# One constant row written on chip instead of sent, and the mask transfers moved behind a weight load, in a one-core attention and feed-forward block

## The chip, the cores and the metric

One core of a Trainium2 chip runs the whole block in one launch. The metric is the device time of that core in microseconds; lower is better. The median of three runs before the change is 766.67 us (765.58 to 767.1).

## The reference

The input x is 1024 tokens of 512 features, in float32. The block is two residual steps, each modulated by vectors from a conditioning row c:

```
mod = silu(c) @ wmod, cut into sa, ca, ga, sb, cb, gb
h = layernorm(x) * (1 + ca) + sa
x = x + ga * attention(h)
h = layernorm(x) * (1 + cb) + sb
x = x + gb * ffn(h)
```

`attention` has 32 heads. Queries come from a latent of 128 numbers per token (RMS-normalised), keys and values from a latent of 32, and a rotary part of 64 numbers is shared by all heads on the key side. The scores are causally masked, go through a softmax, and the values are summed and projected back to 512. `ffn` is a gated feed-forward net with integer weights and 1376 hidden features.

## The kernel before

The program for each engine is written out by hand, with semaphores between the engines. SyncE (SP) issues every transfer, in the order in which the function `sp_program` names them; a wait in it holds everything behind it.

The work has these stages. In the input stage (about 12 to 54 us) the eight tiles of 128 tokens are normalised, turned and projected, which makes the latents and the keys. Then the 32 heads are taken as eight groups of four. For the first group a stage of its own (about 60 to 88 us) finds the row maxima of the scores: TensorE (PE) multiplies queries by keys piece by piece (`maxima_part`, L736), and VectorE reduces each piece. The list `FIRST_MAXIMA` gives the order. Before its first piece PE runs eight matmuls whose result nobody uses (`keep_busy`, L780). After that eight windows of about 57 us follow, one per group (from 90 to about 550 us): each computes the scores of its group, takes exponentials and sums values, and beside this finds the maxima of the next group and makes the queries of the group after that. Last come the output projection and the feed-forward net.

Queries are made four heads at a time on all partitions (tile `TQ`) and are then moved by transfers, one per head and per half of the tokens, into `Q`, where the contraction rows 0 to 95 lie on partitions 0 to 95 (`send_queries`, L531). `maxima_part` waits for each head's transfer (`S_.q`). PE takes its work strictly in order.

The causal mask within a diagonal tile is done by the matmul itself: the contraction is made longer by 32 rows, on partitions 96 to 127. Those rows of `KL`, `KH` and of the two parts of `Q` (high and low, `hl` 0 and 1) hold the constants that `mask_rows` makes. Row 96 (`KR`) of `KH` is all ones, and row 96 of the low part of `Q` takes the negated row maxima of the group, one value per query (`send_maxima`, L540, from `NM`), so that the same matmul subtracts them.

The constants come in one small load to `mask_raw`, GpSimd (POOL) casts them to `mask_made` (L1656), and four transfers spread them along the rows: one each for `KL` and `KH` (8 copies of 128 columns per row) and one for each part of `Q` (32 copies) (`send_mask_rows`, L546). `Q` has two slots, for even and odd groups. The odd slot is filled in the first window by two transfers from the even slot (`copy_mask_rows`, L550). `load_weights(1)` (L521 to L523) fetches the weights of group 1 after POOL has finished with those of group 0 (`S_.wl`, L1669). POOL's first instructions are memsets: `ident`, `ones`, two of `eps`, then `oner` (L1643), `twice` (L1645) and further constants.

Of the kernel before, what the change touches and what calls it, by code (L numbers as in the profile page):

```python
# [7 lines left out]
F32 = mybir.dt.float32  # L8
# [6 lines left out]
P = 128  # L15
# [5 lines left out]
KR = 2 * HALF + L  # L21
# [50 lines left out]
def mask_levels():  # L72

    sizes = [2] * (MASK_ROWS * 2 - 3) + [3] * 3
    starts = [sum(sizes[:n]) for n in range(len(sizes))]
    assert sum(sizes) == P - 1
    return list(zip(starts, sizes))


def mask_rows():  # L80

    k = np.zeros((2, L, P), np.float32)
    q = np.zeros((2, L, P), np.float32)
    for n, (start, size) in enumerate(mask_levels()):
        hide, keep = (30, 45) if size == 2 else (20, 32)
        row = (n // MASK_ROWS, 1 + n % MASK_ROWS)  # L90
        for i in range(size):
            q[row + (start + i,)] = -2.0 ** (hide - i * (hide + keep))
            k[row + (start + 1 + i,)] = 2.0 ** (i * (hide + keep))
        k[row + (slice(start + size + 1, P),)] = 2.0 ** ((size - 1) * (hide + keep))
    k[1, 0] = 1.0
    return np.concatenate([k, q]).transpose(1, 0, 2)


# [406 lines left out]
def sp_program(nc, t, out, M, S_):  # L505
    sp = nc.sync

    def wait_free(engine, key):
        engine.wait_ge(S_.free[TURN[key] % 3], freed(key))

    def load_columns(n):
        sp.dma_start(M.mod_c[n], t["wmod_c"][n]).then_inc(S_.wm[n], 16)

    def load_rows(n):
        sp.wait_ge(S_.mc, n + 1)
        sp.dma_start(M.mod_r[n], t["wmod_r"][n]).then_inc(S_.wm[4 + n], 16)

    def load_weights(g):
        if g > 0:
            sp.wait_ge(S_.wl, g)  # L520
        sp.dma_start(M.WP[:], t["wq_pe"][g]).then_inc(S_.w, 16)  # L521
        sp.dma_start(M.WN[:].rearrange("p h r -> p (h r)"), t["wq_nope"][g]).then_inc(S_.w, 16)
        sp.dma_start(M.WK[:].rearrange("p h r -> p (h r)"), t["wk"][g]).then_inc(S_.w, 16)  # L523

    def send_queries(g, hf):
        cols = slice(hf * QB, hf * QB + QB)
        sp.wait_ge(S_.tl, 2 * g + hf + 1)
        if g > 1:
            sp.wait_ge(S_.sc, NEXP * (g - 2) + (FIRST_EXP[4] if hf == 0 else NEXP))
        for h in range(HG):  # L530
            sp.dma_start(M.Q[0:KR, g % 2, :, hf, h, :].bitcast(F32),  # L531
                         M.TQ[h * L:(h + 1) * L, :, :, cols].bitcast(F32)).then_inc(S_.q[hf][h], 16)

    def send_maxima(g):
        wait_free(sp, ("rows", g))
        if g == 0:
            sp.wait_ge(S_.mk, 64)
        if g == 1:
            sp.wait_ge(S_.mq, 32)
        sp.dma_start(M.Q[KR:KR + 1, g % 2, 1].rearrange("p f h (n q) -> p (f h n) q", q=P).bitcast(F32),  # L540
                     M.NM[:].bitcast(F32)).then_inc(S_.nd, 16)

    def send_mask_rows(kind, dst, done):

        n = dst.shape[1] // P
        sp.dma_start(dst.rearrange("p (n q) -> p n q", q=P).bitcast(F32),  # L546
                     M.mask_made[KR:P, kind, :].bitcast(F32).unsqueeze(1).broadcast_to([P - KR, n, P])).then_inc(done, 16)

    def copy_mask_rows(hl, done):
        sp.dma_start(M.Q[KR:P, 1, hl].rearrange("p f h q -> p (f h q)").bitcast(F32),  # L550
                     M.Q[KR:P, 0, hl].rearrange("p f h q -> p (f h q)").bitcast(F32)).then_inc(done, 16)

    def load_wo(m):
        if m >= 2:
            sp.wait_ge(S_.side, TURN[("fold", G - 1, m - 2)] + 1)
        sp.dma_start(M.WO[m % 2], t["wo"][m].rearrange("p (h d) -> p h d", h=HG)).then_inc(S_.wo[m % 2], 16)
# [26 lines left out]
    sp.dma_start(M.sin[:], t["sin"]).then_inc(S_.tables, 16)  # L583
    load_rows(0)
    load_rows(1)
    sp.wait_ge(S_.mm, 1)
    send_mask_rows(0, M.KL[KR:P, :], S_.mk)
    send_mask_rows(1, M.KH[KR:P, :], S_.mk)
    for hl in range(2):
        send_mask_rows(2 + hl, M.Q[KR:P, 0, hl].rearrange("p f h q -> p (f h q)"), S_.mk)  # L590
    load_weights(1)
    send_queries(0, 0)
    send_queries(0, 1)
    send_queries(1, 0)
# [1 line left out]
    for w in range(G):  # L596
        if w < G - 2:
            load_weights(w + 2)
        if w < G - 1:
            send_queries(w + 1, 1)  # L600
        if w == 0:
            sp.wait_ge(S_.pj, NS)
            sp.wait_ge(S_.nd, 16)
            for hl in range(2):
                copy_mask_rows(hl, S_.mq)
        if w < G - 2:
            send_queries(w + 2, 0)
        if w == G - 2:
            for hf in range(2):
                for h in range(HG):  # L610
                    sp.wait_ge(S_.q[hf][h], 16 * G)
            sp.dma_start(M.x1, t["x"].rearrange("(n p) d -> p n d", p=P)).then_inc(S_.xr, 16)
            sp.dma_start(M.WVF[:], t["wv"]).then_inc(S_.wv, 16)
            load_wo(0)
            load_wo(1)
            load_columns(2)
            load_columns(3)
        if w < G - 1:
            send_maxima(w + 1)
# [26 lines left out]
def pe_program(nc, M, PS, S_):  # L646
    pe = nc.tensor
# [25 lines left out]
    def project_inputs(st):  # L673
        b = st % 2
        pe.wait_ge(S_.hi, st + 1)
        pe.wait_ge(S_.wah, 1)
        if st >= 2:
            pe.wait_ge(S_.cr, st - 1)
        if st == 0:
            pe.wait_ge(S_.lo, 1)  # L680

        terms = [(M.hH[:, st], M.WAH), (M.hL[st], M.WAH), (M.hH[:, st], M.WAL)]
        if st > 0:
            terms = [terms[0], terms[2], terms[1]]
        for n, (h, w) in enumerate(terms):
            if n == (2 if st == 0 else 1):
                pe.wait_ge(S_.wal, 1)
            if st > 0 and n == 2:
                pe.wait_ge(S_.lo, st + 1)
            for k in range(KD):  # L690
                pe.matmul(PS[:, 2 + b, 0:ROWS], h[:, k, :], w[:, k, :], start=(n == 0 and k == 0), stop=False)
        pe.wait_ge(S_.one, 1)
        pe.wait_ge(S_.bias, 2)
        ins = pe.matmul(PS[:, 2 + b, 0:ROWS], M.oner[:], M.bias[:], start=False, stop=True)
        ins.then_inc(S_.pj, 1)
# [16 lines left out]
    def fold_nope(g):  # L712
        bank = side_bank(TURN[("w", g)])
        pe.wait_ge(S_.w, 48 * (g + 1))
        for h in range(HG):
            ins = pe.matmul(bank[:, h * L:(h + 1) * L], M.WN[:, h, :], M.WK[:, h, :], start=True, stop=True)
        ins.then_inc(S_.side, 1)
# [12 lines left out]
    def maxima_part(g, k):  # L730
        qt, lo, w, h0, n = PARTS[k]
        bank = side_bank(TURN[("part", g, k)])
        qs = slice(qt % 4 * P, qt % 4 * P + P)
        for i in range(n):
            pe.wait_ge(S_.q[qt // 4][h0 + i], 16 * (g + 1))
            ins = pe.matmul(bank[:, i * w:(i + 1) * w], M.Q[0:KR, g % 2, 0, qt // 4, h0 + i, qs],  # L736
                            M.KH[0:KR, lo:lo + w], start=(i == 0), stop=(i == n - 1))
        ins.then_inc(S_.side, 1)
# [21 lines left out]
    def side(key):  # L760
        kind, g = key[0:2]
        if kind == "w":
            fold_nope(g)
        elif kind in ("even", "odd", "lat"):
            project_queries(kind, g, key[2])
        elif kind == "part":
            maxima_part(g, key[2])
        elif kind == "rows":
            maxima_rows(g)
        elif kind == "den":  # L770
            denominator(g, key[2])
        elif kind == "modrow":
            mod_rows(key[2], side_bank(TURN[key])).then_inc(S_.side, 1)
        elif kind == "fold":
            fold_values(key[2])
# [62 lines left out]
            side(key)  # L838
    for key in FIRST_QUERIES[1]:
        side(key)  # L840
    pe.wait_ge(S_.cr, NS)
    for key in FIRST_MAXIMA:
        if key == ("part", 0, 0):
# [400 lines left out]
def dve_program(nc, M, PS, S_):  # L1244
    dve = nc.vector
# [27 lines left out]
    def shift_twice():  # L1273

        dve.wait_ge(S_.mc, 2)
        dve.wait_ge(S_.one, 2)
        dve.tensor_copy(M.twice[:, :, 0:L + 1:L], M.mod_col[:, 1, :].unsqueeze(2).broadcast_to([P, KD, 2])).then_inc(S_.tw, 1)

    def mod_late(n, d):
# [353 lines left out]
def pool_program(nc, M, S_):  # L1633
    pool = nc.gpsimd
# [5 lines left out]
    pool.affine_select(out=M.ident[:], in_=M.ident[:], compare_op=ALU.not_equal, fill=1.0,  # L1640
                       base=0, pattern=[[-1, P]], channel_multiplier=1).then_inc(S_.const, 1)
    pool.wait_ge(S_.const, 5)
    pool.memset(M.oner[:].bitcast(F32), 1.0).then_inc(S_.one, 1)  # L1643
    pool.wait_ge(S_.one, 1)
    pool.memset(M.twice[:], 0.0).then_inc(S_.one, 1)  # L1645
    pool.wait_ge(S_.one, 2)
    pool.memset(M.identb[:], 0.0).then_inc(S_.mask, 1)
    pool.memset(M.NMa[:], -MASKED).then_inc(S_.mask, 1)
    pool.memset(M.NMb[:], -MASKED).then_inc(S_.mask, 1)
# [203 lines left out]
```

## Time and profile before

| | |
|---|---|
| median of three runs | 766.67 us |
| the profiled execution's own time | 766.67 us |
| its span, first to last instruction | 764.5 us |
| PE busy | 731.0 us (96%) |
| VectorE (DVE) busy | 542.0 us (71%) |
| ScalarE (ACT) busy | 326.7 us (43%) |
| GpSimd (POOL) busy | 215.4 us (28%) |
| the chain that ended last | PE 69%, DVE 25% |
| transfers, all 16 DMA engines | 63.15 MB, 30.3% of their time |
| granted TensorE clock, mean | 0.997 |

A busy share is a mean over stages that have different limits. A transfer has two times: how long SP was occupied to issue it, and how long from its issue until the last of it landed. The DMA share of a stretch is the sum of the time that its packets took, over 16 engines; packets overlap a little, so it can pass 100%.

### The profile page before, as it was taken

How to read it: one execution, taken by the hardware profiler on the slowest of the kernel's cores; microseconds unless marked ns; L12 is line 12 of the kernel's file. 1: busy time of each engine (PE TensorE's matmuls, PEld its weight loads, DVE VectorE, ACT ScalarE, POOL GpSimd, SP SyncE). 2: the span in 40 equal slices, each digit the busy share in tenths (PEclk: the TensorE clock that was granted, in tenths of full speed). 3: DMA queues.
4: the chain of work that ended last, by engine and by line, in shares of the span. 5: the costliest groups of instructions: out<-in, count | busy, mean ns of one | idle time of the engine just before them, and what ended most of it. 6: DMA issues, size and time to landing. Idle time of an engine off the chain costs nothing.

```text
span 764.5 us, 10504 instructions
## 1 busy us (share of the span) xinstructions
PE 731.0 (96%) x3867; PEld 509.8 (67%) x3867; DVE 542.0 (71%) x803; ACT 326.7 (43%) x499; POOL 215.4 (28%) x196
## 2 busy tenths in 40 slices
PE   3989999999999999999999999999999999999998
PEld 2856676666666666666666666555788888887886
DVE  6867678888888888888888889688695333223432
ACT  4744455545545545545545544444254322222210
POOL 1137635235235235225226121010264000000211
PEclk9999999999999999999999999999999999999999
DMA  8934553303303403303403390360200421200011
GB/s 312 250 72 94 120 118 84 89 11 84 88 12 83 93 7 84 90 11 84 97 3 83 84 358 1 111 220 1 82 23 7 123 71 54 76 10 1 29 41 42
DMA packets 39057, 63.15 MB, mean 83 GB/s; under 512 B 4384, under 2 KB 19232, under 8 KB 37152
## 3 DMA queue, kind: packets, MB, share of 16 engines
q1 hardware_dynamic: 39008, 62.49, 30.3%
q8 instruction: 32, 0.52, 0.3%
q14 instruction: 17, 0.14, 0.1%
HBM read 32.72 MB, written 2.10 MB: 46 GB/s over the span
## 4 chain that ended last, share of the span: by engine, by line
PE 69%; DVE 25%; issue 3%; ACT 2%; DMA 1%; POOL 0%; SPq 0%; DVEq 0%; ACTq 0%; POOLq 0%
PE PS L907 16%; PE PS L924 8%; PE PS L736 8%; DVE PR L1461 7%; PE PS L799 6%; PE PS L817 6%; PE PS L806 5%; PE PS L802 5%; PE PS L871 5%; DVE NMa L1369 4%; DVE wide L1461 3%; PE PS L727 3%; DVE NMd L1374 2%; PE PS L749 2%; PE PS L780 1%
## 5 line engine op out<-in xcount | busy, mean ns | idle before, releaser
L1117 ACT ACTIVATE PR<-PS 128x1024 f32<-128x1024 f32 (+1 forms) x144 | 133.2, 930 | 147.7 <-PE PS L806 116.3
L736 PE MATMUL PS<-KH,Q 96*128 96x128 f32 (+3 forms) x576 | 130.5, 327 | 10.9 <-DVE NMa L1369 5.3
L1369 DVE TENSOR_REDUCE NMa<-PS 128x1 f32<-128x512 f32 (+3 forms) x184 | 116.5, 656 | 29.3 <-PE PS L736 27.4
L736 PEld LDWEIGHTS PS<-KH,Q 96*128 96x128 f32 x576 | 88.8, 190 | 67.3 <-issue 30.7
L799 PE MATMUL PS<-Q,KH 96*128 96x512 f32 x288 | 119.2, 414 | 0.0
L1461 DVE TENSOR_TENSOR PR<-PR 128x2048 f32<-128x2048 f32 (+3 forms) x56 | 112.0, 2000 | 3.9 <-ACT PR L1117 1.5
L806 PE MATMUL PS<-Q,KH 97*128 97x512 f32 (+1 forms) x288 | 114.5, 398 | 0.0
L802 PE MATMUL PS<-Q,KL 96*128 96x512 f32 (+1 forms) x288 | 114.2, 396 | 0.0
L1703 POOL TENSOR_SCALAR_AFFINE_SELECT diag<-diag 128x512 f32<-128x512 f32 x64 | 47.6, 743 | 198.0 <-ACT diag L1062 197.9
L799 PEld LDWEIGHTS PS<-Q,KH 96*128 96x128 f32 x288 | 54.8, 190 | 27.7 <-issue 14.3
L817 PE MATMUL PS<-PR,V 128*32 128x512 f32 (+3 forms) x704 | 70.2, 486 | 0.0
L1585 DVE SCALAR_TENSOR_TENSOR wide<-PS,ffn_s,TQ 128x1024 f32<-128x1024 f32 x10 | 12.8, 1283 | 72.2 <-PE PS L907 72.2
L806 PEld LDWEIGHTS PS<-Q,KH 97*128 97x128 f32 (+1 forms) x288 | 54.6, 190 | 13.2 <-DMA Q<-NM 0.4
L802 PEld LDWEIGHTS PS<-Q,KL 96*128 96x128 f32 (+1 forms) x288 | 54.7, 190 | 8.3
L1062 ACT ACTIVATE diag<-PS 128x512 f32<-128x512 f32 x64 | 38.0, 594 | 46.3 <-PE PS L736 46.3
L907 PE MATMUL PS<-Q 128*128 128x512 f32 x240 | 55.5, 389 | 0.0
L1716 POOL TENSOR_TENSOR wide<-wide,RD 128x512 f32<-128x512 f32 x16 | 34.6, 2164 | 67.4 <-DVE RD L1400 67.4
L1777 POOL TENSOR_TENSOR OT<-TQ,Y 128x512 f32<-128x512 f32 x7 | 9.1, 1294 | 156.7 <-DVE Y L1606 156.7
L907 PEld LDWEIGHTS PS<-Q 128*128 128x128 f32 x240 | 45.0, 188 | 9.3
L907 PE MATMUL PS<-Q,KH 128*128 128x512 f32 (+1 forms) x192 | 49.1, 391 | 0.0
L1374 DVE TENSOR_REDUCE NMd<-diag 128x4 f32<-128x512 f32 x64 | 43.1, 674 | 0.0
L924 PE MATMUL PS<-DH,Q 128*128 128x512 f32 (+1 forms) x176 | 42.6, 390 | 0.0
(185 smaller groups left out, 1088.3 us busy)
## 6 DMA issues: line engine op xcount, KB each, us to landing
Q<-TQ SPq DMA_DIRECT2D x64, 384.0 KB, 6.2
RT<-in_wo SPq DMA_DIRECT2D x4, 1024.0 KB, 4.9
TQ<-in_wo SPq DMA_DIRECT2D x4, 1024.0 KB, 4.8
WI<-in_gate_w SPq DMA_DIRECT2D x10, 256.0 KB, 3.4
WI<-in_up_w SPq DMA_DIRECT2D x10, 256.0 KB, 3.8
DI<-in_down_w SPq DMA_DIRECT2D x10, 256.0 KB, 2.8
PR<-in_wmod_c SPq DMA_DIRECT2D x2, 1024.0 KB, 6.3
x_in<-in_x SPq DMA_DIRECT2D x8, 256.0 KB, 9.7
```

Source lines behind the costliest of these rows:

```text
L736: ins = pe.matmul(bank[:, i * w:(i + 1) * w], M.Q[0:KR, g % 2, 0, qt // 4, h0 + i, qs], M.KH[0:KR, lo:lo + w], start=(i == 0), stop=(i == ...
L799: pe.matmul(dst, M.KH[0:KR, ks], M.Q[0:KR, w % 2, 0, qb, :, qs], start=True, stop=False)
L802: pe.matmul(dst, M.KL[0:rows, ks], M.Q[0:rows, w % 2, 0, qb, :, qs], start=False, stop=False)
L806: ins = pe.matmul(dst, M.KH[0:rows, ks], M.Q[0:rows, w % 2, 1, qb, :, qs], start=False, stop=True)
L817: ins = pe.matmul(PS[h * L:(h + 1) * L, 4, QB - wd:QB], M.V[:, kt, :], M.slot(s)[:, h, 0:wd], start=(kt == 0), stop=(kt == blocks_of(qb) - 1))
L907: ins = pe.matmul(PS[0:m, 4 * b + 2 * w + hf, :], a[b][:, w, k, 0:m], h[:, k, hf * 512:(hf + 1) * 512], start=(n == 0 and k == 0), stop=(n ...
L924: ins = pe.matmul(PS[:, 4 + b, :], a[b][0:k, ch, :], w[0:k, ch, :], start=(n == 0 and ch == 0), stop=(n == 2 and rest == 1))
L1117: act.activation(tiles, banks, ACT.Exp).then_inc(S_.p, 1)
L1369: dve.tensor_reduce(dst, PS[:, bank_of(turn), 0:n * w].rearrange("p (h k) -> p h k", k=w), axis=AX.X, op=ALU.max, negate=True).then_inc(S_ ...
L1374: dve.tensor_reduce(M.NMd[:, qt // 4, :, qt % 4], M.diag[:, qt % 2], axis=AX.X, op=ALU.max, negate=True).then_inc(S_.dm, 1)
L1461: dve.tensor_tensor(sums, sums, M.slot(s)[:, :, 0:wd], ALU.add).then_inc(S_.ad, 1)
L1703: pool.affine_select(out=tile, in_=tile, compare_op=ALU.is_ge, fill=MASKED, base=0, pattern=[[0, HG], [-1, P]], channel_multiplier=1).then ...
```

## The change

- The row of ones is no longer part of the constants that are sent. POOL writes it with a memset of one partition and 1024 columns, put ahead of the memset of `oner`; the semaphore `one` now counts to 3, and its waits are raised by one. SP and PE wait for the first count before the queries are sent and before the maxima begin.
- Row 96 is left out of three sets of transfers: the one to `KH` and the one to the low part of `Q` now start at partition 97, and so does the copy of the low part of `Q` to its odd slot. They carry 31 rows in place of 32. Those of `KL` and of the high part of `Q` stay at 32.
- `send_maxima` no longer waits for the mask transfers; the copy to the odd slot waits for them (`mk`, 64) in place of the first maxima (`nd`, 16).
- `load_weights(1)` stands ahead of the four mask transfers in SP's order, not behind them.

```diff
-    k[1, 0] = 1.0
 ...
     def send_maxima(g):
         wait_free(sp, ("rows", g))
-        if g == 0:
-            sp.wait_ge(S_.mk, 64)
-        if g == 1:
-            sp.wait_ge(S_.mq, 32)
 ...
     def send_mask_rows(kind, dst, done):
+        lo = P - dst.shape[0]
         n = dst.shape[1] // P
         sp.dma_start(dst.rearrange("p (n q) -> p n q", q=P).bitcast(F32),
-                     M.mask_made[KR:P, kind, :].bitcast(F32).unsqueeze(1).broadcast_to([P - KR, n, P])).then_inc(done, 16)
+                     M.mask_made[lo:P, kind, :].bitcast(F32).unsqueeze(1).broadcast_to([P - lo, n, P])).then_inc(done, 16)
     def copy_mask_rows(hl, done):
-        sp.dma_start(M.Q[KR:P, 1, hl].rearrange("p f h q -> p (f h q)").bitcast(F32),
-                     M.Q[KR:P, 0, hl].rearrange("p f h q -> p (f h q)").bitcast(F32)).then_inc(done, 16)
+        lo = KR + hl
+        sp.dma_start(M.Q[lo:P, 1, hl].rearrange("p f h q -> p (f h q)").bitcast(F32),
+                     M.Q[lo:P, 0, hl].rearrange("p f h q -> p (f h q)").bitcast(F32)).then_inc(done, 16)
 ...
     load_rows(1)
+    load_weights(1)
     sp.wait_ge(S_.mm, 1)
     send_mask_rows(0, M.KL[KR:P, :], S_.mk)
-    send_mask_rows(1, M.KH[KR:P, :], S_.mk)
+    send_mask_rows(1, M.KH[KR + 1:P, :], S_.mk)
     for hl in range(2):
-        send_mask_rows(2 + hl, M.Q[KR:P, 0, hl].rearrange("p f h q -> p (f h q)"), S_.mk)
-    load_weights(1)
+        send_mask_rows(2 + hl, M.Q[KR + hl:P, 0, hl].rearrange("p f h q -> p (f h q)"), S_.mk)
+    sp.wait_ge(S_.one, 1)
     send_queries(0, 0)
 ...
         if w == 0:
             sp.wait_ge(S_.pj, NS)
-            sp.wait_ge(S_.nd, 16)
+            sp.wait_ge(S_.mk, 64)
 ...
     pool.wait_ge(S_.const, 5)
+    pool.memset(M.KH[KR:KR + 1, :].bitcast(F32), 1.0).then_inc(S_.one, 1)
+    pool.wait_ge(S_.one, 1)
     pool.memset(M.oner[:].bitcast(F32), 1.0).then_inc(S_.one, 1)
-    pool.wait_ge(S_.one, 1)
+    pool.wait_ge(S_.one, 2)
     pool.memset(M.twice[:], 0.0).then_inc(S_.one, 1)
```

## Rows read from the trace of the kernel before

**Rows 1.** The page: busy times, and the chain that ended last.

```profile
PE 731.0 (96%) x3867; PEld 509.8 (67%) x3867; DVE 542.0 (71%) x803; ACT 326.7 (43%) x499; POOL 215.4 (28%) x196
PE 69%; DVE 25%; issue 3%; ACT 2%; DMA 1%; POOL 0%; SPq 0%; DVEq 0%; ACTq 0%; POOLq 0%
```

**Rows 2.** SP's issues in order of time: start, us that it took, line, transfer.

```profile
14.93 0.73 SPq L546 DMA_DIRECT2D KL<-mask_made  x1
15.70 0.61 SPq L546 DMA_DIRECT2D KH<-mask_made  x1
16.35 10.52 SPq L546 DMA_DIRECT2D Q<-mask_made  x2
33.17 0.33 SPq L521 DMA_DIRECT2D WP<-in_wq_pe  x1
34.10 0.60 SPq L523 DMA_DIRECT2D WK<-in_wk  x1
49.26 31.80 SPq L531 DMA_DIRECT2D Q<-TQ  x12
88.81 0.56 SPq L540 DMA_DIRECT2D Q<-NM  x1
92.31 4.87 SPq L531 DMA_DIRECT2D Q<-TQ  x4
97.27 3.97 SPq L550 DMA_DIRECT2D Q<-Q  x2
118.49 4.86 SPq L531 DMA_DIRECT2D Q<-TQ  x4
```

**Rows 3.** The transfers by kind: count, KB of each, median us from issue to landing.

```profile
Q<-TQ SPq DMA_DIRECT2D x64, 384.0 KB, 6.2
Q<-mask_made SPq DMA_DIRECT2D x2, 512.0 KB, 19.8
KL<-mask_made SPq DMA_DIRECT2D x1, 128.0 KB, 14.9
```

**Rows 4.** The DMA packets between 30 and 34 us (mask transfers only).

```profile
DMA packets 1374, 0.70 MB, mean 175 GB/s; under 512 B 19, under 2 KB 1373, under 8 KB 1373
q1 hardware_dynamic: 1373, 0.69, 118.6%
```

**Rows 5.** The DMA packets between 89.4 and 90.3 us (the one transfer Q<-NM).

```profile
GB/s 0 0 0 0 0 0 0 0 0 0 0 0 0 0 0 0 0 0 0 0 0 0 0 0 0 0 0 23 114 91 137 114 46 91 68 23 23 0 0 0
DMA packets 48, 0.02 MB, mean 18 GB/s; under 512 B 16, under 2 KB 48, under 8 KB 48
q1 hardware_dynamic: 48, 0.02, 7.6%
```

**Rows 6.** The DMA packets between 22 and 24 us (loads to 128 partitions).

```profile
DMA packets 137, 0.86 MB, mean 428 GB/s; under 512 B 13, under 2 KB 13, under 8 KB 52
```

**Rows 7.** PE in order of time at the start of the first maxima.

```profile
58.60 1.90 PE L780 MATMUL PS<-identb 128*128 128x512 bf16 x8
60.15 0.70 PE L736 MATMUL PS<-KH,Q 96*128 96x384 f32 x2
60.73 1.26 PE L736 MATMUL PS<-KH,Q 96*128 96x384 f32 x5
66.13 0.51 PE L736 MATMUL PS<-KH,Q 96*128 96x512 f32 x1 [0.23 <-DVE NMa L1369]
```

**Rows 8.** POOL in order of time, its first memsets and the mask cast.

```profile
1.66 0.21 POOL L1643 MEMSET oner<- 128x128 f32 x1
1.93 0.53 POOL L1645 MEMSET twice<- 128x512 f32 x1
2.86 0.29 POOL L1651 TENSOR_SCALAR_AFFINE_SELECT identb<-identb 128x128 bf16<-128x128 bf16 x1
12.14 0.61 POOL L1656 CAST mask_made<-mask_raw 32x512 fp32r<-32x512 f32 x1 [8.98 <-DMA mask_raw<-in_mask_rows]
```

**Rows 9.** DVE's first use of `twice`.

```profile
13.94 0.17 DVE L1277 COPY twice<-mod_col 128x8 f32<-128x8 f32 x1
```

**Rows 10.** PE, the first piece of the maxima in the second window.

```profile
146.33 0.51 PE L736 MATMUL PS<-KH,Q 96*128 96x384 f32 x2
```

**Rows 11.** Busy us of each engine in two stretches; the eighth figure is PE's granted clock.

```profile
60.00:64.00 4.00, 3.88 (x22) 2.73 (x21) 2.35 (x5) 1.20 (x2) 1.76 (x3) 1.00 0.89 182
466.00:469.00 3.00, 3.00 (x9) 2.32 (x8) 2.63 (x4) 0.28 (x1) 0.06 (x1) 0.50 0.02 5
```

More of the change, by code:

```diff
@@ L691, in project_inputs @@
                 pe.matmul(PS[:, 2 + b, 0:ROWS], h[:, k, :], w[:, k, :], start=(n == 0 and k == 0), stop=False)
-        pe.wait_ge(S_.one, 1)
+        pe.wait_ge(S_.one, 2)
         pe.wait_ge(S_.bias, 2)
@@ L840, in pe_program @@
         side(key)
+    pe.wait_ge(S_.one, 1)
     pe.wait_ge(S_.cr, NS)
@@ L1275, in shift_twice @@
         dve.wait_ge(S_.mc, 2)
-        dve.wait_ge(S_.one, 2)
+        dve.wait_ge(S_.one, 3)
         dve.tensor_copy(M.twice[:, :, 0:L + 1:L], M.mod_col[:, 1, :].unsqueeze(2).broadcast_to([P, KD, 2])).then_inc(S_.tw, 1)
@@ L1642, in pool_program @@
     pool.wait_ge(S_.const, 5)
+    pool.memset(M.KH[KR:KR + 1, :].bitcast(F32), 1.0).then_inc(S_.one, 1)
+    pool.wait_ge(S_.one, 1)
     pool.memset(M.oner[:].bitcast(F32), 1.0).then_inc(S_.one, 1)
-    pool.wait_ge(S_.one, 1)
+    pool.wait_ge(S_.one, 2)
     pool.memset(M.twice[:], 0.0).then_inc(S_.one, 1)
-    pool.wait_ge(S_.one, 2)
+    pool.wait_ge(S_.one, 3)
     pool.memset(M.identb[:], 0.0).then_inc(S_.mask, 1)
```

## The prediction

> **What bounds the kernel now.** I read the page first: PE is busy for 96% of the span and makes 69% of the chain that ended last, DVE 25%, transfers 1% [rows 1]. So what the change does to transfers matters only where PE comes to wait for one. The next view is SP's order of issues [rows 2]. Here the reader sees three things: the mask transfers go out from 14.93 us, while the loads of the input stage still run; the weights of group 1 follow at 33.17 us; the queries of group 0 are issued from 49.26 us. The third view is PE at the start of the first maxima [rows 7]. It uses head 0 at 60.15 us, straight behind the `keep_busy` matmuls. The five matmuls from 60.73 us are one piece of head 2 and the diagonal piece of all four heads, so about 61.1 us is the first time that head 3 is needed. The issue of head 3 starts some three issues after 49.26, each about 1.2 us (4.87/4), and lands 6.2 us later [rows 2, 3]: 49.26 + 3.7 + 6.2 = 59.1 us. The spare time ahead of PE is therefore only 2 us. Whatever makes these queries later than that is paid by PE in full, since PE does its work in order and everything after stands behind this wait.
>
> **The memset and the counts of `one`: nothing.** `oner` (128 columns) took 0.21 us and `twice` (512) 0.53 us [rows 8], so a column costs 0.32/384 = 0.83 ns and 1024 columns about 0.95 us. `twice` is ready near 3.4 us in place of 2.5; DVE uses it at 13.94 us [rows 9], and POOL then waits 8.98 us for the mask constants anyhow [rows 8]. If that cover were gone it would cost 0.95 us. The waits of SP and PE on `one` are passed some 40 us after the count. The waits taken out of `send_maxima` had long been met (`mk` by about 38 us, 17.0 + 20, against 88.81).
>
> **`load_weights(1)` ahead of the masks.** It doesn't come earlier, for it waits for POOL's work on group 0 and is issued at 33.17 us either way. What moves is the mask transfers: from 14.93 us to 34.10 + 0.60 = 34.7 us. With 16 engines on them they would need about as long as now: 160 packets per engine (16 for `KL`, 16 for `KH`, 64 for each part of `Q`; a packet is 512 B), at the pace of rows 4, which is 4 us x 16 / 1373 = 47 ns per packet and engine: 7.5 us. They would be through at about 44 us, ahead of the queries at 49.26. So the move alone costs nothing; it removes the cover of about 20 us that the masks have had.
>
> **31 rows in place of 32.** This is the part that decides. The window with one transfer alone, Q<-NM, holds this [rows 5]: 32 packets of 512 B, and 16 small ones, one for each DMA engine, which report the end. So a transfer of 32 rows is put on all 16 engines, two rows each. Every transfer in the kernel before has 32, 64, 96 or 128 rows on its outer side (or those 32 pieces); none has 31, so the trace doesn't show what happens to one. I bound it from both sides. If the rows may be dealt unevenly, 15 engines get two and one gets one, and the cost is 0. If only equal shares are dealt, 31 is prime and one engine gets all 31. I take the second end: the equal shares of rows 5 are all that the trace has, and no row shows an uneven one.
>
> The Trainium skill, "DMA: Bandwidth & Descriptors", section "Why a DMA increments its semaphore by 16 and not by 1", says the same outright: the number of engines is the largest one up to 16 that divides the slowest dimension of both sides, and its example of 127 partitions runs on one engine. No transfer of this trace tests it. By it the sum is the one below; by uneven shares there would be no difference at all.
>
> Price of a packet on an engine that works alone: that window gives 7.6% of 16 x 0.9 us = 1.09 us for 48 packets [rows 5], so 23 ns if small and large cost alike, 34 ns if the small ones cost nothing. Large packets give 428/16 = 26.8 GB/s per engine [rows 6], which is 19 ns for 512 B. The upper end is 47 ns, the pace when all 16 engines crowd on the same 32 partitions [rows 4]. I take 28, between 23 and 34, since one engine alone has no such crowd.
>
> The one engine then gets: 16 (`KL`) + 31 x 8 = 248 (`KH`) + 64 (high part of `Q`) + 31 x 32 = 992 (low part) = 1320 packets x 28 ns = 37.0 us. The first packet moves about 1.2 us after the issue (in rows 5 at 89.4 + 27 x 0.0225 = 90.0, issued at 88.81): 34.7 + 1.2 + 37.0 = 72.9 us.
>
> The queries are queued behind this on the same engine. SP itself is held too: the second transfer of `Q` took it 10.52 - 0.6 = 9.9 us to issue, and it was let go at 26.9 us, when hardly any of the 160 mask packets of an engine can have moved (`KL`, the first, lands at 14.93 + 14.9 = 29.8). So I let it go with 160 packets left, 4.5 us before the end, at 68.4 us. Head 3 is then issued at 68.4 + 3.7 = 72.1 and lands 6.2 us later, at 78.3 us. Check from the engine's side: 72.9 + 4 heads x 24 KB / 26.8 GB/s = 3.7, plus some 0.8 for the report: 77.4. I take 78.3. PE needs head 3 at 61.1: the delay is 78.3 - 61.1 = 17.2 us.
>
> What is late next: the second half's queries follow at 73.3 us and their first head lands near 79.5; PE wants it at 66.13 + 17.2 = 83.3 [rows 7]. So nothing is added. DVE has its first three reductions done by then (under 1 us won), and PE restarts after 17 us idle; the trace shows that its granted clock can stand at 0.50, the 1.2 GHz level, for 3 us [rows 11], which would cost up to 1.5 us here. These two I set against each other. Sum: +17 us.
>
> **The copy to the odd slot.** Its low part is also 31 rows, of 16 KB each: 31 x 16384 B / 26.8 GB/s = 19 us on one engine, up to twice that in a crowd. Issued at 97.27 (before the shift), with its forerunners through by about 103, it ends at 122; the queries issued at 118.49 land by about 129. PE wants them at 146.33 [rows 2, 10], and the odd slot's rows about then as well. Hidden by 17 us; with that cover gone it would be paid directly. SP's other issues of the first window move with the shift.
>
> The execution that was profiled took 766.67 us, 2.2 more than its span, and equals the median. So 766.67 + 17 = 783.7 us.
>
> **Rivals.**
> 1. Uneven shares: the masks end near 44 us and nothing waits. For: 15 engines with two rows would be the natural way to deal. Against: no such transfer in the trace. 766.7 us, not slower. It decides from the moment 31 rows are put on more than about 3 engines: 1240/3 x 28 ns = 11.6 us, plus 2.2 for the rest, ends at 50, in time for the queries.
> 2. One engine at the crowded pace: 1320 x 47 ns = 62 us, end at 98, head 3 at 98 + 3.7 + 0.8 = 102.5, delay 41 us: 808 us. For: the same partitions are read and written. Against: rows 5 read and wrote just such 512 B pieces at 23 to 34 ns.
> 3. The copy comes late as well: with 16 KB packets at twice the time it ends at 103 + 39 = 142, the queries behind it land at 148 to 150, 2 to 4 us after PE wants them: 783.7 + 3 = 787 us.
>
> **Chances.** Forecast 0.72, rival 1 0.09, rival 2 0.12, rival 3 0.07. The forecast's own range is 776 to 793: 23 ns per packet takes 6.6 us off, 34 ns adds 7.9. For the whole I take 774 to 803, which leaves out rival 1, most of rival 2 and the tails. About 0.2% (1.5 us) is what a measurement can tell from no change. Faster than that 0.02 and the same 0.07, both out of rival 1; slower 0.91.
>
> **What would show it.** The transfers of `KH` and of the low part of `Q` land far later than their forerunners; PE idles some 12 to 17 us just ahead of its first L736, and the wait is put down to the transfer Q<-TQ; the DMA share between 45 and 70 us is about 1/16. SP's issue of the last mask transfer takes over 25 us. After that every stage has its old length. I am wrong if L736 starts near 60 us (shares are uneven), if the idle is near 40 us (the pace), or if a second wait stands at the start of the second window (the copy).

## The result, and the profile after

The changed kernel takes 784.93 us (784.84 to 785.29, 4 runs) against 766.12 us before (4 runs): ratio 1.0245, 95% interval 1.0227 to 1.0263, so 18.8 us slower. The forecast was 783.7 us, with a range of 774 to 803. The profiled execution took 786.67 us with a span of 784.3.

The page of the changed kernel: busy times, the chain by engine, and the group of L733, which is L736 of before; the last line is that group on the page of before. PE's busy time grows by 3.3 us only [rows 1]. The idle time ahead of the group grows from 10.9 to 27.3 us, and 16.6 us of it are ended by a transfer of queries. The chain has an SP share, which was 0% before.

```profile
PE 734.3 (94%) x3867; PEld 512.6 (65%) x3867; DVE 542.3 (69%) x803; ACT 326.6 (42%) x499; POOL 216.2 (28%) x197
PE 66%; DVE 24%; SPq 3%; issue 3%; ACT 2%; DMA 2%; POOL 1%; DVEq 0%; ACTq 0%; POOLq 0%
L733 PE MATMUL PS<-KH,Q 96*128 96x128 f32 (+3 forms) x576 | 134.0, 334 | 27.3 <-DMA Q<-TQ 16.6
```

```profile
L736 PE MATMUL PS<-KH,Q 96*128 96x128 f32 (+3 forms) x576 | 130.5, 327 | 10.9 <-DVE NMa L1369 5.3
```

SP's issues after (start, us, line, transfer), to be read beside [rows 2]. The masks now go out from 34.28 us. The first transfer of queries starts to be issued at 48.83, as before, but SP needs 21.47 us for it.

```profile
33.57 0.67 SPq L521 DMA_DIRECT2D WK<-in_wk  x1
34.28 0.72 SPq L541 DMA_DIRECT2D KL<-mask_made  x1
35.04 0.77 SPq L541 DMA_DIRECT2D KH<-mask_made  x1
35.86 7.49 SPq L541 DMA_DIRECT2D Q<-mask_made  x2
48.83 21.47 SPq L529 DMA_DIRECT2D Q<-TQ  x1
118.61 3.40 SPq L546 DMA_DIRECT2D Q<-Q  x2
```

The DMA packets of the changed kernel between 50 and 60 us. 369 packets in 10 us are one every 27 ns, their time is 7.2% of 16 engines (one engine alone would be 6.25%, and packets overlap a little), and the rate is 19 GB/s: one engine works and 15 are idle.

```profile
DMA packets 370, 0.21 MB, mean 21 GB/s; under 512 B 0, under 2 KB 369, under 8 KB 369
q1 hardware_dynamic: 369, 0.19, 7.2%
```

PE in order of time after, beside [rows 7]. It is ready at 60.1 us as before and uses head 0 at 75.41. The fourth row of L733 is the last head (head 3), at 79.65. Before, it was used at 61.71: the last line is the last of the five matmuls of before, seen alone. So PE is 17.9 us late here.

```profile
58.20 1.90 PE L777 MATMUL PS<-identb 128*128 128x512 bf16 x8
75.41 0.66 PE L733 MATMUL PS<-KH,Q 96*128 96x384 f32 x1 [15.31 <-DMA Q<-TQ]
76.78 0.66 PE L733 MATMUL PS<-KH,Q 96*128 96x384 f32 x1 [0.71 <-DMA Q<-TQ]
77.86 1.20 PE L733 MATMUL PS<-KH,Q 96*128 96x384 f32 x4
79.65 0.48 PE L733 MATMUL PS<-KH,Q 96*128 96x128 f32 x1 [0.59 <-DMA Q<-TQ]
```

```profile
61.71 0.28 PE L736 MATMUL PS<-KH,Q 96*128 96x128 f32 x1
```

The chain of waits after, in order of time, shows the same from the other end: SP holds the chain for 21.5 us, two further issues follow, and the transfer of the last head takes 7.15 us.

```profile
48.83 21.47 SPq L529
70.34 0.61 SPq L529
71.00 1.42 SPq L529
72.46 7.15 DMA Q<-TQ
79.65 0.48 PE PS L733
```

Stretches of 4 us after (the eighth figure is PE's granted clock, then the DMA share and GB/s), beside [rows 11]. PE is idle from 60.1 us; the clock stands at 0.50, the 1.2 GHz level, from about 65 to 89 us. With it a matmul of L733 of 512 columns takes 0.63 us or more, where it took 0.39 to 0.59 at the full clock.

```profile
56.00:60.00 4.00, 4.00 (x19) 1.86 (x18) 1.80 (x2) 2.94 (x5) 0.63 (x1) 1.00 0.07 19
64.00:68.00 4.00, 0.00 (x0) 0.00 (x0) 0.00 (x0) 0.00 (x0) 0.00 (x0) 0.66 0.07 19
72.00:76.00 4.00, 0.59 (x1) 0.29 (x1) 0.00 (x0) 0.00 (x0) 0.00 (x0) 0.50 0.95 213
84.00:88.00 4.00, 4.00 (x14) 2.93 (x13) 2.10 (x4) 1.19 (x2) 2.28 (x3) 0.50 0.38 85
88.00:92.00 4.00, 3.21 (x14) 1.94 (x12) 2.86 (x5) 1.20 (x2) 3.73 (x4) 0.86 0.00 0
```

By the end of this stage the lag has grown to 21.3 us: `send_maxima(0)` is issued at 110.14 us (88.81 before). From there on nothing is added: `send_maxima(1)` is at 163.65 (142.34, 21.3 later) and `send_maxima(6)` at 449.44 (428.05, 21.4 later). The spans differ by 19.8 us, because the profiled execution of before had a stretch at the low clock near 466 us [rows 11] and this one had none there: `send_maxima(7)` is at 499.45 (479.62, 19.8 later).

### The profile page after: what moved, and what is told of

It reads as the page before. It is cut to its first block, busy times and chain, and to the rows that moved or that the text cites. A ratio compares the mean times of both kernels' runs of the same rounds, so it can differ in the third digit from the quotient of the medians.

```text
span 784.3 us, 10504 instructions
## 1 busy us (share of the span) xinstructions
PE 734.3 (94%) x3867; PEld 512.6 (65%) x3867; DVE 542.3 (69%) x803; ACT 326.6 (42%) x499; POOL 216.2 (28%) x197
## 3 DMA queue, kind: packets, MB, share of 16 engines
q1 hardware_dynamic: 38922, 62.45, 28.6%
## 4 chain that ended last, share of the span: by engine, by line
PE 66%; DVE 24%; SPq 3%; issue 3%; ACT 2%; DMA 2%; POOL 1%; DVEq 0%; ACTq 0%; POOLq 0%
PE PS L905 15%; PE PS L922 8%; PE PS L733 8%; DVE PR L1459 6%; PE PS L796 6%; PE PS L814 6%; PE PS L803 5%; PE PS L799 5%; PE PS L869 5%; DVE NMa L1367 4%; DVE wide L1459 3%; SPq L529 3%; PE PS L724 3%; DVE NMd L1372 2%; PE PS L746 2%
## 5 line engine op out<-in xcount | busy, mean ns | idle before, releaser
L733 PE MATMUL PS<-KH,Q 96*128 96x128 f32 (+3 forms) x576 | 134.0, 334 | 27.3 <-DMA Q<-TQ 16.6
L733 PEld LDWEIGHTS PS<-KH,Q 96*128 96x128 f32 x576 | 92.0, 196 | 83.9 <-issue 47.7
L814 PE MATMUL PS<-PR,V 128*32 128x512 f32 (+3 forms) x704 | 70.2, 486 | 0.0
```

The source lines that it names most:

```text
L814: ins = pe.matmul(PS[h * L:(h + 1) * L, 4, QB - wd:QB], M.V[:, kt, :], M.slot(s)[:, h, 0:wd], start=(kt == 0), stop=(kt == blocks_of(qb) - 1))
```

## The experiments

The kernel before was timed beside each of them, on the same chip; its medians lay between 765.1 and 765.5 us. Ratios are to it.

**e1_rows32: 32 rows again, in the late place.**

```diff
-    send_mask_rows(1, M.KH[KR + 1:P, :], S_.mk)
+    send_mask_rows(1, M.KH[KR:P, :], S_.mk)
-        send_mask_rows(2 + hl, M.Q[KR + hl:P, 0, hl] ...
+        send_mask_rows(2 + hl, M.Q[KR:P, 0, hl] ...
-        lo = KR + hl
+        lo = KR
```

Not shown: the ones come with the constants again, and the waits that the change took out of `send_maxima` and moved for the copy are back.

> The changed kernel with one part undone: the transfers to KH, to the low part of Q and the copy carry 32 rows again (the ones come with the constants again); the late place of the masks and POOL's memset stay. Theory (31 rows go to one DMA engine): masks on 16 engines end near 44 us, first L733 near 60 us, granted clock never low there, 766 us (765 to 767). Rival (the late place behind the weight load is what costs): 785 us, with the 15 us idle of PE still there.

765.54 us, ratio 1.0004 (0.9992 to 1.0017). In its profile the packets between 36 and 45 us move at 144 GB/s on all engines, and PE uses the first head at 60.23 us:

```profile
DMA packets 2589, 1.30 MB, mean 144 GB/s; under 512 B 60, under 2 KB 2589, under 8 KB 2589
58.68 1.90 PE L782 MATMUL PS<-identb 128*128 128x512 bf16 x8
60.23 0.70 PE L738 MATMUL PS<-KH,Q 96*128 96x384 f32 x2
```

The late place alone costs nothing, nor does the memset; the rival falls. That the moved waits cost nothing either is shown by e3_split below, which keeps them as the change has them.

**e2_early31: 31 rows, in the early place.**

```diff
-    load_weights(1)
     sp.wait_ge(S_.mm, 1)
     ... (the four mask transfers)
+    load_weights(1)
     sp.wait_ge(S_.one, 1)
```

> The changed kernel with the other part undone: 31 rows stay, but the masks go out at 15 us again, ahead of the second weight load. Theory: the one engine gets to the masks when the loads ahead are through, near 28 us, and needs 37 us for 1320 packets, so it ends near 65; head 3 of the queries lands near 71 in place of 79; PE is late by about 10 us and the total is 777 us (774 to 780). Rival (late place alone): 766 us. Both parts needed and multiplying, no cost of 31 rows when early: 766 us too.

777.09 us, ratio 1.0146 (1.0122 to 1.0170). The sum was right and the wait named was not, so that the total matches is in part luck. Here the weights of group 1 stand behind the masks: SP needs 27.10 us to issue the first of them, and PE waits for `WK` at L713, ahead of the maxima. By the time it is through, the queries have landed.

```profile
16.78 17.80 SPq L541 DMA_DIRECT2D Q<-mask_made  x2
34.63 27.10 SPq L519 DMA_DIRECT2D WP<-in_wq_pe  x1
67.05 1.89 PE L713 MATMUL PS<-WK,WN 64*128 64x32 f32 x8 [9.52 <-DMA WK<-in_wk]
71.90 0.82 PE L733 MATMUL PS<-KH,Q 96*128 96x384 f32 x2
```

So 31 rows cost 12 us in the early place and 20 in the late one.

**e3_split and e7_17_14: the 31 rows cut in two.** Both send the same bytes in the same number of transfers; the second has 17 in place of the 16. In both the sets of 32 rows go as 16 + 16, and the copies to the odd slot are cut in the same way.

```diff
-        sp.dma_start(dst ... M.mask_made[lo:P, kind, :] ...).then_inc(done, 16)
+        for a, b in ((lo, lo + 16), (lo + 16, P)):
+            sp.dma_start(dst[a - lo:b - lo] ... M.mask_made[a:b, kind, :] ...).then_inc(done, 16)
```

> The changed kernel with each set of 31 rows cut into two transfers, of 16 and of 15 rows (and each of 32 rows into 16 and 16); everything else as changed. Theory (equal shares only): 16 and 15 engines take them, the masks end near 45 us, 766 us (765 to 767). Rival (partition 97 as a start, or the odd place itself, is what makes it slow, not the row count): 780 us or more.

> As e3_split, the same bytes in the same number of transfers, but the 31 rows are cut as 17 + 14 in place of 16 + 15. Theory (equal shares only, so a prime number of rows over 16 goes to one engine): 17 rows on one engine, 14 rows on 14; that engine gets 16 + 136 + 8 + 64 + 544 + 32 = 800 packets, 23 us at the 28.9 ns measured, its last mask packet starts near 58.5 us, head 3 lands some 7 us later near 66, and the total is 5 us over before: 770.5 us (769 to 773). Rival (rows are dealt as evenly as they go, and 31 was slow for being odd, or for its bytes): 765 us, as e3_split.

16 + 15: 765.28 us, ratio 1.0003 (0.9991 to 1.0016). 17 + 14: 775.41 us, ratio 1.0128 (1.0111 to 1.0145). The packets between 50 and 56 us, first of 16 + 15, where all engines are already at the queries, then of 17 + 14, where one engine still moves mask packets of 512 B (222 in 6 us, 27 ns each):

```profile
DMA packets 631, 1.22 MB, mean 204 GB/s; under 512 B 41, under 2 KB 41, under 8 KB 630
q1 hardware_dynamic: 630, 1.21, 90.0%
```

```profile
DMA packets 223, 0.13 MB, mean 22 GB/s; under 512 B 0, under 2 KB 222, under 8 KB 222
q1 hardware_dynamic: 222, 0.11, 7.2%
```

One row more in one transfer costs 10 us. That is neither the odd number (15 is odd) nor the start at partition 97. The time of 17 + 14 is 5 us over its expectation. The transfer of the 14 rows stands right behind that of the 17, and SP is held in its issue from 42.84 to 57.65 us. So its packets start only then, and packets of 512 B are still moving until about 62.7 us, where 58.5 was expected for the last. Head 3 is used at 69.20 where 66 was expected, and the low clock lasts from 65 to 79 us.

```profile
39.15 18.51 SPq L543 DMA_DIRECT2D Q<-mask_made  x4
42.84 14.81 SPq L543 DMA_DIRECT2D Q<-mask_made  x1
69.20 0.47 PE L736 MATMUL PS<-KH,Q 96*128 96x128 f32 x1 [0.22 <-DMA Q<-TQ]
```

**e6_half: half of the columns of the low part as 31 rows.**

```diff
+            send_mask_rows(3, low[KR + 1:P, 0:half], S_.mk)
+            for a, b in ((KR + 1, KR + 17), (KR + 17, P)):
+                sp.dma_start(low[a:b, half:] ... M.mask_made[a:b, 3, :] ...).then_inc(S_.mk, 16)
```

> The changed kernel, but of the low part of Q only the first half of the columns goes as 31 rows (16 copies, 496 packets); the second half goes as 16 and 15 rows. The one engine keeps 16 + 248 + 64 + 496 + 31 = 855 of 1320 packets. Theory (price per packet, 37 us / 1320): its masks end 13.6 us earlier, near 60 us, head 3 lands near 66 in place of 79.6, PE hardly idles long enough for a low clock, and the total is 5 us over before: 770 us (769 to 773). Rival (a 31-row transfer has a large fixed price, or SP's hold is what counts): 780 us or more.

776.71 us, ratio 1.0151 (1.0137 to 1.0165). The direction holds, the sum doesn't: SP is let go at 57.8 us, head 3 is used at 70.03, not 66, and the clock is low from 65 to 75. The half with 16 and 15 rows is issued behind the half with 31, and SP is held in the issue of the 16 rows from 43.73 to 56.84 us.

```profile
43.73 14.08 SPq L595 DMA_DIRECT2D Q<-mask_made  x2
43.73 13.11 SPq L595 DMA_DIRECT2D Q<-mask_made  x1
57.93 33.33 SPq L529 DMA_DIRECT2D Q<-TQ  x12
70.03 0.48 PE L742 MATMUL PS<-KH,Q 96*128 96x128 f32 x1 [0.25 <-DMA Q<-TQ]
```

Head 3 is used 9.6 us sooner than in the changed kernel for 465 packets fewer on the engine, 21 ns for each, below the 27 to 29 of the packets themselves. So beside the part that grows with the packets there is one of about 3 us that the expectation didn't have. Part of it is seen: the 16 + 15 rows could start only when SP was let go, and packets of 512 B moved until about 61.5 us, where 60 was expected. The rest isn't explained.

**e8_gate: is it the crowd?** One more wait on SP, so that the 15 engines cannot run ahead into the second half's queries.

```diff
     send_queries(0, 0)
+    sp.wait_ge(S_.q[0][HG - 1], 16)
     send_queries(0, 1)
```

> The changed kernel with one more wait on SP: the second half's queries of group 0 are issued only when head 3 of the first half has landed. In e6_half and e7_17_14 six to eight us passed between the last mask packet and head 3, where 3.7 + 0.8 were worked out. Theory (the other 15 engines run ahead into the second half and crowd the one that is late): with the wait the late engine moves its 48 query packets at 84 ns, head 3 is used near 78.3 us in place of 79.65, and the total is between 783.5 and 786, since the second half then comes a little late. Rival (the time goes to something else, as SP's issue): head 3 at 79.5 as before, total 786 us or more.

786.1 us, ratio 1.0259 (1.0238 to 1.0280); head 3 is used at 79.26 us. The theory falls: the wait brought 0.4 us at most. From the release of SP at 70.2 us to head 3 there are the issues of heads 1 and 2 and then the transfer of head 3, 6.89 us, not far from the 6.2 us of an ordinary one [rows 3].

```profile
79.26 0.48 PE L734 MATMUL PS<-KH,Q 96*128 96x128 f32 x1 [0.38 <-DMA Q<-TQ]
```

```profile
72.33 6.89 DMA Q<-TQ
```

**e9_kh31 and e5_copy31: one engine, but in time.** In the first only the transfer to `KH` has 31 rows, in the second only the copy in the first window. The other transfers have 32 again, by the lines of e1_rows32: the first takes its second and third pair of lines, the second its first and second.

> Only the transfer to KH carries 31 rows, late as in the changed kernel; both parts of Q and the copies carry 32. The one engine gets 16 + 248 + 64 + 64 = 392 packets, some 13 us, and is through near 48.5 us, just ahead of the queries issued at 48.8. Theory: nothing waits, as before within 0.2% (765 to 766.5). Rival (any transfer on one engine at this place costs): 768 us or more.

> Only the copy of the low part to the odd slot carries 31 rows; the four mask transfers carry 32. Theory: the copy takes one engine some 20 us in the first window, ends 20 us ahead of its need, and costs nothing: as before within 0.2%. Rival (it holds the next queries until PE wants them): 3 us or more over before.

`KH` alone: 765.53 us, ratio 0.9999 (0.9987 to 1.0010). The copy alone: 765.66 us, ratio 1.0011 (1.0002 to 1.0020), that is 0.46 us in the medians and at most 0.2%. Its packets between 108 and 117 us: 15 in 9 us, 16 KB each, 0.60 us apiece, so 31 take 19 us on the one engine and nobody waits.

```profile
DMA packets 15, 0.25 MB, mean 27 GB/s; under 512 B 0, under 2 KB 0, under 8 KB 0
```

**e4_busy, a0_after and e4_again: the low clock.**

```diff
         if key == ("part", 0, 0):
-            keep_busy(3, 8)
+            keep_busy(3, 72)
```

> The changed kernel with 72 in place of 8 unused matmuls ahead of the first piece of the maxima: PE works from 58 to about 74 us and hardly idles. The queries come no earlier. Theory: what the low clock after the wait costs (head 3 is 18.5 us late, everything after 21.3 us) goes, so 782 us (781 to 783.5). Rival (the 2.8 us come from something else, as the order in which the heads land): 785 us.

e4_busy took 785.46 us (783.63 to 786.41), but its profiled execution was 2.4 us shorter than that of the changed kernel. So it was run again, beside the unaltered changed kernel:

> The changed kernel unaltered, timed on the same chip as the three beside it: 784 us (783 to 786), the yardstick for e4_again.

> The kernel of e4_busy again (72 unused matmuls ahead of the maxima), now beside the changed kernel on one chip, since its profile was 2.4 us shorter than that of the changed kernel while its timed runs (783.6 to 786.4) were not. If the low clock after the wait costs 2.4 us in every execution: 2 us or more below a0_after. If timed executions lose what the profile shows won, or never had it: within 0.7 us of a0_after.

785.10 us for a0_after (ratio 1.0265, 1.0251 to 1.0279) and 784.81 us for e4_again (1.0263, 1.0249 to 1.0277): no difference that can be told. With the added work the clock stays up through the wait, but it still falls for some 3 us behind it, from about 79.5 to 83 us. Three stretches of e4_again:

```profile
72.00:76.00 4.00, 2.63 (x12) 0.97 (x9) 0.30 (x1) 0.00 (x0) 0.00 (x0) 1.00 0.94 213
76.00:80.00 4.00, 1.82 (x9) 1.35 (x9) 1.37 (x3) 0.00 (x0) 0.00 (x0) 0.94 0.91 228
80.00:84.00 4.00, 4.00 (x19) 3.48 (x18) 1.89 (x4) 1.19 (x2) 2.12 (x3) 0.63 0.91 220
```

The spans are 784.3 and 782.4 us for two profiles of the changed kernel, 781.9 and 782.0 with PE kept busy. The difference arises in this stage. From the use of head 3 to `send_maxima(0)` it was 27.1 us before, 30.5 and 28.5 in the two profiles of the changed kernel, and 28.4 in both with PE kept busy. So against these the longer low clock cost about 2.1 us in the one profile and 0.1 in the other, where it lasted 20 us in place of 24. All four have the clock low from about 79.6 to 83 us, and all take at least 1.3 us more than before here; how much of that is the clock isn't shown. In timed runs the gain of the added work isn't separated from nothing.

## Why the prediction was right

**The deciding step** was the choice between uneven shares and one engine, taken without a row that showed it. The runs decide it: 19 GB/s on one engine in the profile after, no loss with 32 rows or with 16 + 15, and 10 us for 17 + 14. The Trainium skill's rule ("DMA: Bandwidth & Descriptors", "Why a DMA increments its semaphore by 16 and not by 1") says that the number of engines is the largest divisor up to 16; this case shows it for 31 and 17 (one engine) and, by the time, for 16 + 15.

**Price of a packet:** taken as 28 ns; 27 where the engine is alone. SP begins the masks at 34.28 us. Packets of 512 B move until about 73.3 us, where 72.9 was worked out: with 1.2 us for the first, 28.6 ns for each of the 1320. Two stretches show the end, 73.0 to 73.5 and 73.5 to 74.0 us; 13 packets are between 512 B and 2 KB in the first, one in the second (a packet of the queries is larger).

```profile
DMA packets 68, 0.10 MB, mean 194 GB/s; under 512 B 11, under 2 KB 24, under 8 KB 68
DMA packets 51, 0.10 MB, mean 202 GB/s; under 512 B 1, under 2 KB 2, under 8 KB 51
```

**When SP is let go:** at 70.3 us, where 68.4 was worked out. That is 3.0 us ahead of the end, with some 110 packets left (an estimate: 3.0 us at 27 ns each), not 4.5 us and 160 packets.

**Where SP is held** was wrong. The prediction held it in the issue of the last mask transfer; in fact all four were issued by 43.35 us (35.86 + 7.49), and the first transfer of queries took the 21.47 us. The time is nearly the same, since the first transfer of queries stands next in line behind the last mask transfer. The sign named for it (over 25 us at the last mask) didn't appear.

**Arrival of head 3:** worked out 78.3, measured 79.65: 1.9 us from the release of SP, 1.0 from the landing (7.15 in place of 6.2 us), less 1.5 from the issues before it (2.2 in place of 3.7, since the held issue is itself the first of the three). PE's need of head 3 in the kernel before was read as about 61.1 us; the trace has 61.71. So the delay is 17.9 us, where 17.2 was worked out. (The expectation of e4_busy still goes by 61.1: its 18.5 and 2.8 us are 17.9 and 3.4.)

**Second half, restart:** nothing was late next, as said. The gain of DVE and the low clock were set against each other, as nothing. That term was too small: in the profiled execution 3.4 us were lost (21.3 in place of 17.9), in a0_after 1.4 (19.4 in place of 18.1). Span for span the sum is 17.9 + 3.4 - 1.5 (the stretch near 466 us, which only before had) = 19.8 us.

**The total is closer than the sum.** The forecast added 17 us to 766.67 us, an execution that has the stretch at low clock near 466 us. Timed beside the experiments the kernel before takes 765.1 to 765.5 us, and the changed one on the same chip 785.10 against 765.20: 19.9 us. The sum of +17 is 3 us short of that; that 783.7 lies only 1.2 us from 784.93 is in part luck. The mechanism is right: one engine, and PE's wait for queries queued behind it.

**The move, the memset, the copy:** costed at nothing, measured at nothing by e1_rows32; the copy at 0.5 us at most by e5_copy31. But the prediction read the move as a mere loss of cover; e2_early31 shows that in the early place the same 37 us hold up another user, the weights of group 1, so that place costs 12 us too.

**The rivals:** uneven shares fell with the one engine at 19 GB/s, the crowded pace (47 ns) with the 27 ns. The late copy fell with 0.60 us per 16 KB packet and with PE's waits: none for a transfer of queries came after that of head 3, up to 300 us.

No version tried is faster than the kernel before: 16 + 15 rows with the memset is as fast.

## What to carry to other kernels

Look at the row count of every transfer before its bytes: dropping one of 32 rows saved 3% of the bytes and put all of them on one engine. For the 31 rows here the cure was to cut them in two, 16 + 15; 17 + 14 was none, since 17 has no divisor up to 16 but 1 either. What such a transfer costs is read not from itself but from the first user behind it in the same queue, and from how much time lies between: the copy of 31 rows took 19 us on one engine and was free, since nobody needed its rows before the second window.

## What was not expected of the hardware

One engine's backlog stops SP, though 15 engines are empty. In all four kernels the held issue is that of the transfer right behind the large one on one engine, whatever it carries: the first queries in the changed kernel (21.47 us), the weights in e2_early31 (27.10), the 16 rows in e6_half (13.11), the 14 rows in e7_17_14 (14.81). It happens behind the 31 rows of `KH` too: the high part of `Q`, issued next, took 4.37 us in the changed kernel, where with 32 rows (e1_rows32) both parts together took 1.35.

```profile
35.86 4.37 SPq L541 DMA_DIRECT2D Q<-mask_made  x1
35.92 1.35 SPq L546 DMA_DIRECT2D Q<-mask_made  x2
```

How much backlog an engine may have before SP stops wasn't tried.

After PE's wait of some 15 us the granted clock stayed at the 1.2 GHz level for 24 us in one profile and for 20 in another of the same kernel, though PE was at work again for the last 14 and 8 of them.
